# One VectorE instruction for the eight one-hot matrices of a group, in place of eight

## The reference

```
h = relu(layernorm(x))
messages = concat(h[src], edge_attr) @ W_message
agg = segment_sum(messages, dst)
t = layernorm(relu(agg) + h) * scale + bias
n = three-layer MLP of 256 x 256 with skip connections (t)
out = x + layernorm(h + n) * scale + bias
```

## Time and profile before

| | us |
|---|---|
| median of 3 runs (lowest, highest) | 2287.95 (2285.52, 2295.1) |
| the profiled execution | 2290.32 |
| its span | 2288.5 |
| TensorE matmuls busy | 1681.2 |
| GpSimd busy | 1591.7 |
| VectorE busy | 952.6 |
| ScalarE busy | 366.6 |
| mean granted clock of TensorE | 0.937 |

### The profile page before, as it was taken

How to read it: one execution, slowest core, us unless ns; L and a number is a source line. 1 busy time by engine, 2 the same in 40 slices (tenths; PEclk the granted TensorE clock), 3 DMA queues, 4 the chain that set the end, 5 groups by cost and what they waited for, 6 DMA issues and landing times.

```text
span 2288.5 us, 35804 instructions
## 1 busy us (share of the span) xinstructions
PE 1681.2 (73%) x6729; PEld 1128.3 (49%) x6730; DVE 952.6 (42%) x3949; ACT 366.6 (16%) x1114; POOL 1591.7 (70%) x1673
## 2 busy tenths in 40 slices
PE   0027778877778877778778778887777877778876
PEld 0015555555545545545545555555554555545554
DVE  7444344344434434434434433444343334434434
ACT  2321111111111111111111111111111111111112
POOL 0037777777777777777777777777777777777771
PEclk9999999899999999999999989989999989999987
DMA  9875555555555555555555555555555555555542
GB/s 181 248 203 157 149 161 155 148 160 156 150 160 156 150 158 157 150 157 158 152 158 156 151 160 156 155 154 157 151 156 159 157 151 156 158 150 155 160 123 64
DMA packets 409301, 357.80 MB, mean 156 GB/s; under 512 B 276832, under 2 KB 355488, under 8 KB 409120
## 3 DMA queue, kind: packets, MB, share of 16 engines
q0 software_dynamic: 79872, 218.21, 33.8%
q1 hardware_dynamic: 268784, 82.79, 15.5%
q10 hardware_dynamic: 60464, 55.28, 7.6%
HBM read 329.65 MB, written 26.48 MB: 156 GB/s over the span
## 4 chain that ended last, share of the span: by engine, by line
POOL 45%; PE 22%; issue 19%; DMA 3%; DVE 3%; DVEq 1%; ACT 1%; POOLq 0%; ACTq 0%
POOL ring L284 45%; PE acc_banks L364 12%; DMA ring<-h_table,src_all 3%; PE agg_bank L316 3%; PE agg_bank L322 2%; PE y_bank L298 2%; PE z_bank L298 2%; DVE onehot L673 1%; PE acc_banks L372 1%; DVEq L220 1%; ACT r_bank L414 0%; PE z_bank L308 0%; PE st_bank L333 0%; DVE scaled L510 0%; DVEq L673 0%
## 5 line engine op out<-in xcount | busy, mean ns | idle before, releaser
L284 POOL DMA_INDIRECT ring<-h_table,src_all x1664 | 1590.6, 956 | 648.0 <-issue 637.7
L364 PE MATMUL acc_banks<-ring,onehot 128*128 128x320 f32 x3328 | 1117.0, 483 | 538.4 <-issue 236.8
L364 PEld LDWEIGHTS acc_banks<-ring,onehot 128*128 128x128 f32 x3328 | 657.7, 209 | 958.1 <-issue 799.2
L673 DVE TENSOR_SCALAR onehot<-iota,dst_rel 128x128 f32<-128x128 f32 x1664 | 357.3, 300 | 257.2 <-issue 202.5
L483 DVE TENSOR_TENSOR w<-agg_bank,h_late 128x256 f32<-128x256 f32 x103 | 43.7, 424 | 955.6 <-PE agg_bank L322 955.6
L402 ACT ACTIVATE uT<-z_bank,fp 128x128 f32<-128x128 f32 x200 | 80.7, 454 | 1482.9 <-PE z_bank L308 1482.9
L316 PE MATMUL agg_bank<-wm,ST 128*128 128x256 f32 (+1 forms) x594 | 167.4, 403 | 0.0
L316 PEld LDWEIGHTS agg_bank<-wm,ST 128*128 128x128 f32 (+1 forms) x594 | 108.2, 195 | 56.3 <-issue 36.5
L322 PE MATMUL agg_bank<-wl,u 128*128 128x256 f32 x408 | 118.1, 413 | 6.3 <-DVE z L521 6.3
L298 PEld LDWEIGHTS y_bank<-u,wl 128*128 128x128 f32 x808 | 107.6, 194 | 5.5
L414 ACT ACTIVATE r_bank<-y_bank,fp 128x128 f32<-128x128 f32 x202 | 60.6, 338 | 297.7 <-PE y_bank L298 297.7
(11 more groups left out here) (108 smaller groups left out, 872.5 us busy)
## 6 DMA issues: line engine op xcount, KB each, us to landing
ring<-edges SPq DMA_DIRECT2D x208, 256.0 KB, 4.4
ring<-h_table,src_all POOLq DMA_INDIRECT x1664, 2.8
h_late<-h_table ACTq DMA_DIRECT2D x103, 128.0 KB
x_late<-x ACTq DMA_DIRECT2D x103, 128.0 KB
h_in<-h_table ACTq DMA_DIRECT2D x100, 128.0 KB
xs<-x SPq DMA_DIRECT2D x14, 896.0 KB, 7.5
h_table<-xs SPq DMA_DIRECT2D x14, 896.0 KB, 5.0
out<-o ACTq DMA_DIRECT2D x98, 128.0 KB
```

The source lines that it names most:

```text
L284: nc.gpsimd.indirect_dma_start(out=ring[:, k * GT + j, 0:D], out_offset=None, in_=h_table, in_offset=bass.IndirectOffsetOnAxis(ap=src_all[ ...
L364: return nc.tensor.matmul(acc_of(at), onehot[:, (k % OG) * GT + j, :], ring[:, k * GT + j, :], start=False, stop=True, skip_group_check=True)
L673: op = nc.vector.tensor_scalar(onehot[:, (k % OG) * GT + j, :], iota[:, :], dst_rel[:, bass.ds(g * GT + j, 1)], None, ALU.is_equal)
```

## The change

In the group loop of VectorE one tensor_tensor of 128 x (8 x 128) elements takes the place of eight tensor_scalar of 128 x 128. Its first operand is iota, repeated eight times (a zero stride over the tile), its second the eight columns of dst_rel, each element repeated 128 times (a zero stride over the lane). The comparison, the output and the place of the semaphore's increment are those of before.

```
-                        for j in range(GT):
-                            op = nc.vector.tensor_scalar(onehot[:, (k % OG) * GT + j, :], iota[:, :],
-                                                         dst_rel[:, bass.ds(g * GT + j, 1)], None, ALU.is_equal)
-                        op.then_inc(onehots, 1)
+                        slot = (k % OG) * GT
+                        keys_of = dst_rel[:, bass.ds(g * GT, GT)].rearrange("p (j q) -> p j q", q=1).to_broadcast([P, GT, P])
+                        lanes_of = iota[:, :].rearrange("p (q n) -> p q n", q=1).to_broadcast([P, GT, P])
+                        nc.vector.tensor_tensor(onehot[:, slot:slot + GT, :], lanes_of, keys_of, ALU.is_equal).then_inc(onehots, 1)
```

## The result

The changed kernel took 2377.59 us (median of 4, 2375.71 to 2381.89), the kernel before beside it 2286.73 us (2282.66 to 2295.1): ratio 1.0395, 95% interval 1.0362 to 1.0428. It is 90.9 us slower; the forecast was 2382, 94 us above the 2287.95 from which it started. The profiled execution took 2375.71 us, 85.4 more than that of before.

A forecast was written before the change was run, and what follows sets the result against it. GpSimd's gathers were taken to bound the kernel. The profiled 2290.3 us plus 100 for held gathers less 6 for old delays gave 2384, less 2.4 to the median: 2382 us, range 2345 to 2425.

The forecast's parts named there:

- What bounds: Main loop: GpSimd's 1664 gathers set the pace at 1.261 us each, 2097 us in all, never waiting for the array.
- The build's length: VectorE's one-hot build per group: one two-input instruction of 1024 elements takes 1.21 us, replacing 1.66 us.
- The gate, stretched fourfold: Gathers beside a build: held while its elements stream, 1.07 us for 1024, scaled from a 256-element row.
- How many and how much: Gathers beside the 208 builds: about 170 stretched, adding 100 us in all.
- random phases: Builds starting at random against the gathers' 1.25 us pitch: 0.46 us per group, 95 us in all.
- the old starts: Gate laid over 199 group starts of the old timeline: 0.53 us per group, 111 us for 208.
- The 6 us of the old builds: Gathers beside the old eight-instruction builds: 98 stretched by 6.0 us in all, which goes away.
- Prologue and tail: Before the first gather and after the last: both stay, at 143 and 48 us.
- The first: Gathers beside builds: left alone by the new instruction, giving 2282 us; chance 6%.
- The second: Array on the path: it gets onehots 0.45 us earlier and gathers are hardly delayed, giving 2268 us; chance 3%.
- The third: Build's repeated operand goes row by row: gate up to 2.18 us, every build delays a gather, 2605 us; chance 3%.
- The fourth: Builds locked to the bad phase of gathers: 0.75 us or more per group, say 2450 us; chance 5%.

The follow-up runs named there:

- e5: Changed kernel with iota read from PSUM and the xb bias from SBUF; 2278.9 us against 2283.75 for the kernel before, ratio 0.998.
- e6: Changed kernel with every build done twice back to back, first into an unread buffer; 2890 us against 3347 for the kernel before.
- e4: Changed kernel with each build in eight two-input instructions of 128 elements; this form's two runs gave 0.995 and 0.999 of the kernel before, not told apart.

## Why the prediction was right

Point by point, by its steps:

- **What bounds.** Right: the added 85.1 us of gathers reappear as 85.0 us of span. The fixed 0.30 us before every gather was the row that told it; the chain's 22% for the array was no bound. The gap is still 0.30.
- **The build's length.** 1.21 forecast from two rows of other sizes, 1.226 measured. No cost of the zero strides shows.
- **The gate, stretched fourfold.** 1.07 us forecast, 1.05 measured: the latest gather that was still held began 1.05 us after the build and took 1.00. Forecast of the longest gather 2.02, measured 1.998; end after the build's start 2.1, measured 2.05.
- **How many and how much.** About 170 forecast, 184 measured. The mean hold per group was put at 0.48 us, between 0.46 for random phases and 0.53 from the old starts; it was 92.0 / 208 = 0.44. This is the term that was off, by 8 us of 100. Where it went, the trace shows. The 123 builds that don't follow another closely cost 0.48 us each, as I had put it. The 85 others start within 1.9 us of the one before (2.4 to 2.8 in the old kernel), and there the phase is not free any more: a held gather ends 2.05 us after the first build's start and the next one begins 0.30 later, at 2.35. A build that follows at 1.5 us meets it 0.84 us after its own start and holds it by 0.24 us (49 of them); one that follows at 1.8 or 1.9 us meets it at 0.51 and holds it by 0.59 (36). All 85 hold a gather, by 0.39 us on average. The plain random figure (95) was nearer than my choice of 100, but by luck: neither it nor the old starts know of this lock.
- **The small terms.** The 6 us of the old builds went. Gathers held by other instructions (L523, L521, L488) took 7.3 us before and 6.0 now. 92.0 - 6.1 - 1.3 = 84.6, which is the difference of the profiled executions (85.4) but for 1 us.
- **How near the time came.** Partly luck. Between the profiled executions the forecast was 94 us and the difference 85.4, and that is the size of the miss. The medians, 90.9 us apart, look better because the profiled execution of before lay 3.6 us above its median and that of the changed kernel 1.9 below.
- **Prologue and tail.** First gather at 143.0 for 142.9; from the end of the last (2324.7 + 0.95) to the span's end 47.9 us for 48.
- **The rivals.** The first (a gather left alone) is dead by the 184 held ones and by e5, which shows about the time that it promised (2279 us, 4.9 below the kernel before where it had 6), but for an operand in PSUM. The second (array on the path) fails by the gaps before gathers, which are still 0.30 us, and by the span, which grew by what the gathers grew; e5 bounds it: with builds 0.45 us shorter and no delay the kernel gained 4.9 us, no more than the 8 us by which its gathers are held less (13.5 us in all before, 5.5 in e5). The third needed a build of 2 us. The fourth needed 0.75 us per group.

The sentence of the Trainium skill on which the first rival rested ("SBUF — State Buffer", "Who interferes with whom": tensor_tensor doesn't stall descriptor generation, inferred) does not hold here: 184 gathers say the opposite. The rule before it, two SBUF inputs against a GpSimd operation that reads SBUF, does, and e5 is its test. The same section of the Trainium skill has the shared ports held for the whole instruction, but says so of the 2-port modes only; the two-input builds here held gathers back for 1.05 us of 1.226.

## What to carry to other kernels

Before merging or lengthening a VectorE instruction, look at what GpSimd does beside it: where its indirect DMAs set the pace, an instruction with two SBUF tensors holds each gather that it meets until it has streamed, so n pieces of the same total delay gathers about 1/n as much (87, some 39 and 8 us for one, two and eight, all on chips where gathers had slack), and one operand in PSUM costs nothing (2279 us for 2378). Pieces that follow each other at a fixed distance can lock to the gathers' pitch, so draw both on one time line before trusting an average over random starts. A count of saved instructions, or of saved VectorE time (102 us of busy time here), says nothing about that. And a verdict belongs to the limit under which it was measured: on a chip where the array halted and gathers had slack, the same change gained 17%.

## What the runs showed of the hardware that I had not expected

- The gate is exact: 128, 512 and 1024 elements gave mean holds of 0.07 to 0.08, 0.25 and 0.50 us, and gathers that started beside a build of 1024 ended 2.04 to 2.05 us after its start, nearly all, whenever they had begun.
- Builds and gathers lock: in e6 doubled builds 2.51 us apart let gathers with a pitch of 1.25 us pass (0.02 us of delay each), and in the changed kernel every one of the 85 builds that followed another within 1.9 us held a gather.
- The same kernel took 2284 to 2287 us on some chips and 3336 to 3459 on others (medians), with a granted TensorE clock of 0.94 and of 0.74 to 0.77. On the slow ones the prologue was the same (first gather at 142.5 to 143.1 us) and a gather too (median 946 to 949 ns); it is the array that halts at "issue" (931 us in e4, 314 in the changed kernel's first profile). What causes it no run here told.
